# Attention's norm and q projection moved one tile forward in a five-engine transformer kernel

## The reference, cut to what matters

```python
def attention(hidden_states, attention_mask, adapter, Wq, Wk, Wv, Wo, gate):
    q = split_heads(hidden_states @ Wq, q_len)
    k = split_heads(hidden_states @ Wk, q_len)
    v = split_heads(hidden_states @ Wv, q_len)
    q = q * cos + _rotate_half(q) * sin
    k = k * cos + _rotate_half(k) * sin
    scores = jnp.einsum('bhqd,bhkd->bhqk', q, k) * inv_sqrt_d + attention_mask
    w = jax.nn.softmax(scores, axis=-1)
    attn_output = jnp.einsum('bhqk,bhkd->bhqd', w, v)
    ...
    return attn_output @ Wo

x = x + jnp.tanh(g_xattn[0]) * attention(_layernorm(x), mask, ctx_2048, ...)   # 32 heads of 8
x = x + jnp.tanh(g_ffn[0]) * experts_of_8_top1(_layernorm(x), ...)
x = x + jnp.tanh(g_xattn[1]) * wkv(w, u, _layernorm(x), ctx_2048)
x = x + jnp.tanh(g_ffn[1]) * experts_of_8_top2(_layernorm(x), ...)
```

## Time and profile before

| | us |
|---|---|
| median of 3 runs | 629.57 (627.92 to 630.57) |
| the profiled execution | 622.23 |
| its span, first to last instruction | 620.4 |
| PE busy | 511.7 (82%), 3103 matmuls |
| PE weight loads | 366.2 (59%) |
| DVE busy | 323.8 (52%) |
| ACT busy | 212.8 (34%) |
| POOL busy | 148.6 (24%) |
| chain that ended last, by engine | PE 60%, DVE 19%, issue 8%, POOL 4%, ACT 3%, DMA 3% |

### The profile page before, as it was taken

How to read it: one execution, slowest core, us unless ns; L and a number is a source line. 1 busy time by engine, 2 the same in 40 slices (tenths; PEclk the granted TensorE clock), 3 DMA queues, 4 the chain that set the end, 5 groups by cost and what they waited for, 6 DMA issues and landing times.

```text
span 620.4 us, 10154 instructions
## 1 busy us (share of the span) xinstructions
PE 511.7 (82%) x3103; PEld 366.2 (59%) x3104; DVE 323.8 (52%) x881; ACT 212.8 (34%) x474; POOL 148.6 (24%) x238
## 2 busy tenths in 40 slices
PE   2587998898987998998969462159999999999994
PEld 1355767566675675775857351136766766666663
DVE  5553678887867787878865526672111111111110
ACT  1717274462642644626512211012222222222220
POOL 3060113023121130130301300022333333333322
PEclk9757999999897998978979756559999999999998
DMA  8600000000000000000000079941122211122211
GB/s 220 194 2 4 1 5 2 5 20 1 22 3 1 21 1 4 17 0 23 2 4 19 1 295 419 336 127 18 26 33 34 34 27 28 30 34 34 30 21 17
DMA packets 24738, 32.79 MB, mean 53 GB/s; under 512 B 5912, under 2 KB 21280, under 8 KB 24704
## 3 DMA queue, kind: packets, MB, share of 16 engines
q1 hardware_dynamic: 19424, 25.80, 12.8%
q0 software_dynamic: 4416, 6.03, 6.3%
q10 hardware_dynamic: 864, 0.54, 0.3%
HBM read 26.60 MB, written 5.24 MB: 51 GB/s over the span
## 4 chain that ended last, share of the span: by engine, by line
PE 60%; DVE 19%; issue 8%; POOL 4%; ACT 3%; DMA 3%; SPq 1%; DVEq 1%; POOLq 0%; ACTq 0%
PE bank_o L1502 10%; PE bank_s L1481 9%; PE bank_t L1481 9%; PE bank_t L1317 5%; PE bank_a L1191 3%; PE bank_o L1273 3%; PE bank_s L1230 2%; DVE X L862 2%; PE bank_b L1491 2%; POOL rstd L392 2%; PE bank_t L1254 2%; PE bank_a L1286 2%; PE bank_t L1260 2%; DMA CT<-in_ctxT 2%; PE bank_t L1255 1%
## 5 line engine op out<-in xcount | busy, mean ns | idle before, releaser
L1502 PE MATMUL bank_o<-w,hT 128*128 (+1 forms) x276 | 67.9, 388 | 0.7 <-DVE hT L1137 0.7
L390 POOL TENSOR_SCALAR rstd<-mv 128x1 f32<-128x1 f32 x32 | 7.2, 224 | 229.5 <-DVE mv L740 229.5
L464 POOL DMA_INDIRECT out_x<-ys,idx_out x23 | 36.8, 1599 | 101.4 <-ACT ys L703 101.4
L1481 PE MATMUL bank_s<-w,xgT 128*128 x184 | 59.9, 470 | 0.6 <-ACT xgT L493 0.6
L1481 PE MATMUL bank_t<-w,xgT 128*128 x184 | 58.2, 459 | 0.0
L1502 PEld LDWEIGHTS bank_o<-w,hT 128*128 128x128 f32 (+1 forms) x276 | 48.7, 189 | 13.5 <-issue 8.5
L806 DVE TENSOR_REDUCE mx<-bank_s 128x8 f32<-128x512 f32 x64 | 43.5, 687 | 24.4 <-PE bank_s L1232 22.8
L1230 PE MATMUL bank_s<-Kh,Qx 128*128 128x128 f32 x256 | 47.1, 313 | 5.7 <-ACT Qx L532 5.7
L555 ACT ACTIVATE Pt<-bank_t 128x512 f32<-128x512 f32 x64 | 37.4, 595 | 40.8 <-PE bank_t L1260 40.8
L1137 DVE COPY hT<-bank_c 128x256 f32<-128x256 f32 x23 | 9.8, 425 | 72.8 <-PE bank_c L1491 72.8
L1481 PEld LDWEIGHTS bank_t<-w,xgT 128*128 128x128 f32 x184 | 35.0, 190 | 19.5
(11 more groups left out here) (233 smaller groups left out, 981.7 us busy)
## 6 DMA issues: line engine op xcount, KB each, us to landing
w<-in_w SPq DMA_DIRECT2D x16, 704.0 KB, 14.0
w<-in_w2T SPq DMA_DIRECT2D x8, 640.0 KB, 8.9
CT<-in_ctxT SPq DMA_DIRECT2D x1, 1024.0 KB, 9.8
Pt<-in_WT SPq DMA_DIRECT2D x1, 1024.0 KB
mrow<-mhl SPq DMA_DIRECT2D x64, 8.0 KB, 1.9
X<-in_x SPq DMA_DIRECT2D x1, 896.0 KB, 7.0
out_x<-X SPq DMA_DIRECT2D x6, 128.0 KB, 1.7
normed<-h SPq DMA_DIRECT2D x6, 128.0 KB, 1.7
```

The costliest lines, as they stand in the source:

```text
L464: pool.indirect_dma_start(out, bass.IndirectOffsetOnAxis(ap=idx_out[:, :], axis=0), ys[:, :], None, compute_op=ALU.add).then_inc(added, 16)
L1481: ins = pe.matmul(o[:, 0:IH], xgT[:, c, :], w13[:, c, bass.ts(e, 1), q, :].rearrange("p o n -> p (o n)"), start=(c == 0), stop=(c == KT - 1))
L1502: ins = pe.matmul(bo[:, 0:HID], hT[0:k, i, :], w2[0:k, i, bass.ts(e, 1), :].rearrange("p o n -> p (o n)"), start=(i == 0), stop=(i == IT - 1))
```

## The change

`over_tiles` counts pairs instead of tiles (the same tiles in the same loop). The norm before attention, its transpose and the q projection of tile t+2 now stand in tile t (for tile 1 in tile 0's turn, and VectorE's norm of tile 1 ahead of all tiles). VectorE runs `ln_stats(0, t+2)` before and `ln_apply(0, t+2)` after `wkv_args`; POOL's `rstd_of(0, t+2)` stands before the wkv products; TensorE runs `turn_hn(t+2)` before `attend(3)` and `project_q(t+2)` after `values(2)`; ScalarE copies both between its last steps of the tile. `rotate_q(t+1)` moves from behind the maximum of unit 7 to behind that of unit 4, `turn_q(t+1)` between row scores 6 and 7, `low_q` ahead of tile t-2's wkv steps. `project_kv(t+1, 0)` moves ahead of `output(t-1)`, and `project_kv(t+1, 1)` ahead of `gate_logits(t-1)`. Tile 6 prepares nothing for t+2, and tile 7 is as it was.

```diff
--- before.py
+++ after.py
@@ -278,9 +278,9 @@
 
             body(0, 0, False, False, True)
             body(1, 1, False, True, True)
-            with eng.Fori(2, NT - 2, 2) as t:
-                body(t, 0, True, True, True)
-                body(t + 1, 1, True, True, True)
+            with eng.Fori(1, NT // 2 - 1) as pair:
+                body(pair * 2, 0, True, True, True)
+                body(pair * 2 + 1, 1, True, True, True)
             body(NT - 2, 0, True, True, True)
             body(NT - 1, 1, True, True, False)
 
@@ -303,6 +303,10 @@
             for j in range(2):
                 after(eng, nd_mul, u, 2, j + 1)
                 eng.tensor_tensor(ND[:, j, :, :], ND[:, j, :, :], VE[:, 1, j, :, :], ALU.add).then_inc(nd_sum, 1)
+
+        def two_on(t, nxt):
+
+            return nxt and not (isinstance(t, int) and t == NT - 2)
 
         class Chain:
 
@@ -421,8 +425,6 @@
             rstd_of(0, 1)
 
             def tile(t, par, prev2, prev, nxt):
-                if nxt and prev:
-                    rstd_of(0, t + 1)
                 if nxt:
                     ctx_of(t + 1)
                     mask_of(t + 1, 1 - par)
@@ -435,6 +437,8 @@
                     rstd_of(3, t - 2)
                 if prev:
                     rstd_of(2, t - 1)
+                if two_on(t, nxt):
+                    rstd_of(0, t + 2)
                 if prev:
                     wkv_products(pool, t - 1)
                     wkv_sums(pool, t - 1)
@@ -625,20 +629,21 @@
             high_w0()
 
             def tile(t, par, prev2, prev, nxt):
-                if nxt:
+                if not prev:
                     evac_hn(t + 1)
                     evac_q(t + 1)
                 if prev:
                     evac_ao(t - 1)
+                if nxt:
+                    evac_v(t + 1, 1 - par, 0)
+                    evac_qT(t + 1)
+                if prev:
                     evac_h2(t - 1)
                     high_h2(t - 1)
                 shifts(t)
-                if nxt:
-                    evac_v(t + 1, 1 - par, 0)
                 if prev:
                     gate(t - 1)
                 if nxt:
-                    evac_qT(t + 1)
                     evac_v(t + 1, 1 - par, 1)
                 if prev:
                     evac_comb(t - 1)
@@ -661,8 +666,12 @@
                     decay(t - 1)
                 attend(t, 2)
                 heads_out(t, 1)
+                if two_on(t, nxt):
+                    evac_hn(t + 2)
                 attend(t, 3)
                 heads_out(t, 2)
+                if two_on(t, nxt):
+                    evac_q(t + 2)
                 heads_out(t, 3)
 
             over_tiles(act, tile)
@@ -939,22 +948,23 @@
             dve.wait_ge(ld_x, 16)
             dve.wait_ge(prep_act, 2)
             dve.wait_ge(ld_ffn, 16 * 8)
+            ln_stats(0, 1)
+            ln_apply(0, 1)
             dve.tensor_scalar(nuc[:, :], uc[:, :], -1.0, None, ALU.mult).then_inc(prep, 1)
             dve.wait_ge(prep, 4)
 
             def tile(t, par, prev2, prev, nxt):
                 u, w = t - 1, t - 2
-                if nxt:
-                    ln_stats(0, t + 1)
                 maxima(t, range(2, 3))
-                if nxt:
-                    ln_apply(0, t + 1)
                 if prev:
                     heads(u, 0)
                 maxima(t, range(3, 4))
                 if prev:
                     heads(u, 1)
-                maxima(t, range(4, 6))
+                maxima(t, range(4, 5))
+                if nxt:
+                    rotate_q(t + 1)
+                maxima(t, range(5, 6))
                 if prev:
                     residual1(u)
                     ln_stats(1, u)
@@ -962,17 +972,15 @@
                 if prev:
                     ln_apply(1, u)
                 maxima(t, range(7, 8))
-                if nxt:
-                    rotate_q(t + 1)
                 shift_low(t)
                 if prev:
                     gate(u)
+                if nxt:
+                    low_q(t + 1)
                 if prev2:
                     wkv_inverse(w)
                 if prev2:
                     wkv_out(w)
-                if nxt:
-                    low_q(t + 1)
                 if prev:
                     mix(u, 0)
                     mix(u, 1)
@@ -994,8 +1002,12 @@
                 if nxt:
                     rotate_k(t + 1, 1)
                     mask_low(t + 1, 1 - par)
+                if two_on(t, nxt):
+                    ln_stats(0, t + 2)
                 if prev:
                     wkv_args(u)
+                if two_on(t, nxt):
+                    ln_apply(0, t + 2)
                 if nxt:
                     low_k(t + 1, 1 - par)
                 if prev:
@@ -1359,27 +1371,29 @@
             pe.wait_ge(ld_ffn, 16 * 8)
 
             def tile(t, par, prev2, prev, nxt):
-                if nxt:
+                if not prev:
                     turn_hn(t + 1)
                 row_scores(t, par, range(4, 5))
-                if nxt:
+                if not prev:
                     project_q(t + 1)
                 if prev:
                     turn_heads(t - 1, True)
                 row_scores(t, par, range(5, 6))
+                if nxt:
+                    project_kv(t + 1, 0)
                 if prev:
                     output(t - 1)
-                row_scores(t, par, range(6, 8))
-                if nxt:
-                    project_kv(t + 1, 0)
+                row_scores(t, par, range(6, 7))
+                if nxt:
+                    turn_q(t + 1)
+                row_scores(t, par, range(7, 8))
                 if prev:
                     turn_h2(t - 1)
                 turn_maxima(t)
+                if nxt:
+                    project_kv(t + 1, 1)
                 if prev:
                     gate_logits(t - 1)
-                if nxt:
-                    turn_q(t + 1)
-                    project_kv(t + 1, 1)
                 if prev:
                     turn_comb(t - 1)
                     experts0(t - 1, 0)
@@ -1405,10 +1419,14 @@
                 values(t, par, 1, prev)
                 if nxt:
                     row_scores(t + 1, 1 - par, range(1))
+                if two_on(t, nxt):
+                    turn_hn(t + 2)
                 attend(t, par, 3, prev)
                 if nxt:
                     row_scores(t + 1, 1 - par, range(1, 2))
                 values(t, par, 2, prev)
+                if two_on(t, nxt):
+                    project_q(t + 2)
                 if nxt:
                     row_scores(t + 1, 1 - par, range(2, 3))
                 values(t, par, 3, prev)
```

More of the change, by code:

```diff
@@ L1369, in tile @@
                 row_scores(t, par, range(5, 6))
-                if prev:
-                    output(t - 1)
-                row_scores(t, par, range(6, 8))
                 if nxt:
@@ L1375, in tile @@
                 if prev:
+                    output(t - 1)
+                row_scores(t, par, range(6, 7))
+                if nxt:
+                    turn_q(t + 1)
+                row_scores(t, par, range(7, 8))
+                if prev:
                     turn_h2(t - 1)
                 turn_maxima(t)
+                if nxt:
+                    project_kv(t + 1, 1)
                 if prev:
                     gate_logits(t - 1)
-                if nxt:
-                    turn_q(t + 1)
-                    project_kv(t + 1, 1)
                 if prev:
```

## The result

The changed kernel takes 645.82 us (median of 4 runs, 645.19 to 646.66) against 628.75 us for the kernel before (4 runs, 625.09 to 630.57): a ratio of 1.028, 95% interval 1.023 to 1.0329. It is slower by 17.1 us; the forecast was 647, range 636 to 659. The profiled execution took 646.66 us (span 644.8), that of before 622.23 (span 620.4): between the two profiles lie 24.4 us, 7 more than between the medians. In the three later sets of runs the kernel before had medians of 626.5, 624.76 and 624.74 us (60 runs, 620.73 to 630.54), so its 628.75 stands high, and the 17.1 us are uncertain by some 4.

The account below looks back on a forecast made before the run. The prediction took the tiles' part as bound by a chain between TensorE and VectorE. Its terms summed to +17.65 us on the profiled 622.23, giving 639.9, carried to the median as 647 us, range 636 to 659.

Parts of the forecast that it names:

- What would show it: Signs: `comb` wait about 1.9 us, h2 wait 1.4 to 1.7, H+7.0 to h2's turn, H to second `attend` 21.5 to 23.
- order, heads to second `attend`, tiles 1 to 6: Moved kv projections delay h2, logits and `comb`; VectorE carries it on: 2.3 us in tiles 2 to 6, 2.1 in tile 1, +13.6.
- before the scans, and the start of tiles: Norm work beside wkv's arguments delays tiles 0 to 5, +2.0 us; the moved q projection and norm cost tile 1 +0.45.
- loop's jump: Where the loop jumps, TensorE no longer waits for the norm: between 0 and 2.6 us back, taken as -1.5.
- tile 0: `project_kv(1, 0)` no longer hides unit 7's maximum, so `turn_maxima` and SP's transfers start later: +1.1 us, range 0 to 2.
- clock, tiles 1 to 6: TensorE's clock may fall with more and longer waits: taken as +2 us, bounds -4.6 and +18.
- the clock falls in both projections: Rival: low clock in both kv projections costs +9 to +13 us instead of +2, about +26, 656 us; chance 0.12.
- The carry-over to the median: The profiled execution lies 7.3 us below the median of 629.57; that difference was taken to carry over, 639.9 becoming 647 us.
- HAM oscillation: Skill's rule: long TensorE waits lower the clock; by it, waits under 2 us cost only themselves, clock term no worse than 0.

Follow-up runs that it names:

- the last run but one: The kernel before with VectorE taking the maximum of unit 2 ahead of the next tile's norm statistics: 629.17 us against 624.74, ratio 1.005.
- The other profiled execution of this order: The kernel before with only its loop counted in pairs, every engine's instruction order unchanged: median 624.45 us against 626.5, profiled execution 629.34 us.

## Why the prediction came out right, and where its steps did not

The direction, the size and the cause (both kv projections moved out of VectorE's shadow onto the chain) are as forecast. Of "What would show it" the waits and the first instruction after the jump came out in every tile. The distances did so at the full clock alone: h2 turned at H+7.02 there, but at H+8.60 to H+9.94 in tiles 2 to 6 of the changed kernel, and of its stretches to the second `attend` only tiles 4 and 6 lie in the 21.5 to 23 us. Four of the terms were mis-sized, and in part they offset each other. Between the two profiled executions:

| term | forecast | measured |
|---|---|---|
| order, heads to second `attend`, tiles 1 to 6 | +13.6 | +13.3 |
| before the scans, and the start of tiles | +2.45 | -0.4 |
| loop's jump | -1.5 | -4.8 |
| tile 0 | +1.1 | +4.75 |
| clock, tiles 1 to 6 | +2 | +10.8 |
| from tile 7 to the end | 0 | +0.8 |
| sum | +17.65 | +24.4 |

- **Order**: right. Tile by tile at the full clock, the new order (its waits filled) takes 19.29, 21.22, 21.02, 21.14, 21.02 and 20.91 us in tiles 1 to 6. The old one takes 17.50 and 19.14 in tiles 1 and 2 of before (71.83 to 89.33, and rows 1), and 18.58, 18.83, 18.60 and 18.63 in tiles 3 to 6 with its waits filled. That is +1.8 in tile 1 (2.1 forecast), +2.1 to +2.4 in the others (2.3 forecast), and +13.3 in all. It is an estimate from three profiles. VectorE did carry the delay on through the mixes.
- **Before the scans, and the start of the tiles**: too high. From the second `attend` to the next turn of the heads are 20.02 us in tile 2 of after (140.75 to 160.77) and 20.06 in that of before (127.74 to 147.80, rows 1); tiles 1, 2, 4, 5 and 6 together take 98.2 against 98.7. The 0.35 us per tile that `ln_stats(0, t+2)` was to take beyond its cover didn't appear.
- **The jump**: the mechanism was right, the size was not. In before the same distance is 24.82 us in tile 3 (167.50 to 192.32, rows 1), in after 20.03. All 4.8 us came back. The prediction bounded the gain at 2.6 and called the 4.55 us of VectorE a cost of "jumps here". No such idle time is left once the norm's statistics don't stand first in VectorE's loop body, as the last run but one shows.
- **Tile 0**: what was forecast came out, and a second cost was missed. With the rotation late the low shift comes at 45.81 against 44.60, close to the +1.1 from "a maximum and its handover". With the rotation early, beside POOL's split, its first two steps take 4.74 us from 38.28 on, instead of some 0.7 clear of POOL. So the low shift comes at 47.73, and `attend` resumes at 54.40 (51.27 before, rows 8). Of the +4.75 at tile 1's H, 2.5 are the rotation's place, by the run that moves it; 1.2 are the forecast delay, and 1.0 comes behind it, where no run separates waits from clock.
- **The clock**: the term that failed. It was taken as +2, "near today's losses, as most of the experts' work stays hidden behind VectorE", with +18 as the bound. Filling the waits takes 17.3 us off the six tiles. From the turn of the heads to the second `attend` the kernel before takes 117.9 us in tiles 1 to 6, and 111.3 by the full-clock times under "Order", so it had lost 6.6 already. That leaves 10.8 for the change, five times the forecast and within the +9 to +13 of the rival "the clock falls in both projections". That rival had its mechanism right in tiles 3 and 5 (3.62 and 3.12 us in tile 3, H to the second `attend` 25.88); in tiles 2, 4 and 6 mainly the first projection is slow. With a chance of 0.12 it came nearer to the difference of the profiles (about +26 against 24.4) than the forecast did.
- **The carry-over to the median**: "the difference carries over" was wrong. The other profiled execution of this order was 7.1 us longer, by low clock in tile 0 and tile 2, which before's profiled execution escaped. The changed kernel has low clock in tile 2 in its profile too, and its four runs lie within 1.5 us. So 17.65 came out near the 17.1 of the medians by luck, because two errors met: the sum was 6.8 us short of the profiled difference, and an offset of 7 us was taken for constant.

The rule of the Trainium skill that was weighed in the prediction (TensorE: Matmul & The Clock Gate, "HAM oscillation") doesn't describe this kernel: no wait of TensorE in tiles 1 to 6 exceeds 1.91 us in after, and yet its clock falls to half in part of each of them. The Trainium skill (TensorE: Matmul & The Clock Gate, "A second HAM failure mode: psum-queue depth-cycling") tells of a kernel whose clock oscillates from short pauses between groups of matmuls. The changed kernel with its waits filled agrees (1.00 in every tile instead of 0.74 to 0.93); the fall at 109 us in the filled kernel before, with TensorE busy, is not covered by it.

## What to carry to other kernels

Where two engines hand work to each other, an independent block of TensorE work belongs behind the handover, where it covers the other engine's chain. Moved ahead of the step that starts that chain it cost its length here, and then more, as waits opened and the clock fell. Where a wait has no work to fill it, try a cheap matmul whose product nobody reads, and judge it by the granted clock over the whole tile, since it gained some 2% in two orders here and nothing in a third. Before a sum made against one profiled execution is carried to a median, find out where the two executions differ.

## What the runs showed of the hardware

- **Short waits and the clock.** Three waits of 1.4 to 1.9 us in each tile go with a granted clock of 0.74 to 0.93 from the heads to the second `attend`; with a matmul of some 1 us put into each, the clock is 1.00 in tiles 1 to 6 and 17.3 us come back. But the clock also fell with TensorE busy since 103.64, at some 109 us of the filled kernel before.
- **VectorE beside POOL.** A two-input operation of VectorE of 0.41 us (128x256) and one of 0.28 (128x128) took 2.46 and 2.44 us beside POOL's two-input operations of 2.35 to 2.54 us (128x1024), each ending just after POOL's did. In the kernel before the first of them, started later in POOL's last operation, took 1.42. The Trainium skill (SBUF — State Buffer, "Who interferes with whom") states that a VectorE instruction with two SBUF inputs contends with a GpSimd instruction that reads SBUF. The rows agree, and show VectorE's held until POOL's ends. The last two of POOL's three operations of the split, from the profile of after:

```profile
38.10 2.35 POOL L410 TENSOR_TENSOR w0l<-AR,w0h 128x1024 fp32r<-128x1024 f32 x1
40.40 2.54 POOL L410 TENSOR_TENSOR w0l<-VE,w0h 128x1024 fp32r<-128x1024 f32 x1
```

- **The jump of a loop.** VectorE idles 4.55 us at the jump, waiting for nothing that the profile shows, where the norm's statistics are the first instruction of the loop body. Where a maximum stands first it idles 0.79 us, for TensorE. Why that instruction and not the other was not tried.
